# Additions to the output between GpSimd's weight splits, and the tiles without rows moved ahead of the fifth expert's

## The chip, the cores and the metric

The kernel runs on one core of one Trainium2 chip. The metric is the device time of one execution in microseconds, lower is better, given as the median of several runs. Profiles show one execution each: TensorE (PE, weight loads PEld), VectorE (DVE), ScalarE (ACT), GpSimd (POOL) and the sync engine (SP), each with its own instruction queue, and 16 DMA engines that all queues share.

## The reference

16 samples of 69 tokens of width 256 (a class token, 36 image patches, 32 text tokens; 1104 tokens) pass a patch embedding, one attention layer and one layer of experts. The last is what the change touches:

```
h = h + ffn(layernorm(h))
ffn(x): shared = expert(x, shared_up, shared_down)              # all tokens
        probs  = softmax(x @ router_w)                          # 8 routed experts
        gates  = the two largest probs of each token, else 0
        routed = sum over e of gates[e] * expert(x, routed_up[e], routed_down[e])
        return shared + routed + x
expert(x, up, down) = gelu(x @ up) @ down                       # 256 -> 1024 -> 256
```

## The kernel before, in words

**Stages.** Patch embedding and attention take the first third. The shared expert runs over all tokens while the router's result is turned into a table. Then the routed experts run over tiles of 128 rows, each row a (token, expert) pair.

**Tiles.** `TILES` is 25, the most that 2208 pairs over 8 experts can need; each expert's rows fill whole tiles, one expert after another. `rtab[:, 1]` is each expert's number of tiles, `rtab[:, 2]` the scan of it (the tile at which each expert ends), `rtab[:, 3]` where it starts. Tiles that no expert needs stand at the end; their rows all point at 128 spare rows behind the output, and their gates are zero. They are computed like the others, with the last expert's weights. `etab` gives each tile its expert, `eplace` the expert's turn in the ring of weights.

**TensorE.** Step `s` of `run_steps` transposes tile s+2's rows, makes tile s+1's up product (L876 to L878 with `xgT`, after a wait on `w_ready` for its expert's turn), turns tile s's hidden values, and makes tile s-1's down product. VectorE multiplies it by the gates into `xy_all[:, t]` (L1418) and raises `y_ready`.

**GpSimd** runs one queue, written out by hand. `prepare_half(x, part)` splits half an expert's weights (up, then down; 2048 elements a partition) from `stage` into a high part (L394) and a low part (L395) in the ring of four experts' places, then issues the load of the next expert's same half (L384). For x above 4 it first waits for the tiles of the expert whose place it takes. x = 0 is the shared expert, x = 1 to 8 the routed ones. `gather_rows` (L502) reads a tile's 128 normalized rows by an indirect DMA; the sync engine then copies them to `xg` (L355), from which TensorE transposes. `add_rows` (L512) adds a tile's results to the output's rows in HBM by an indirect DMA with addition. Two experts may hold the same token, so an addition must not run beside another expert's: `additions[t]` (made on VectorE up to L1370) is the count of `y_out` that it waits for (L509), the end of the experts before its own; a tile without rows waits for all additions before it, since all use the same spare rows. It also waits for its own result (L511). In the kernel before, all 25 additions stand behind the last split.

**VectorE** makes the tables while TensorE works on the shared expert, in a chain in which each instruction waits for the last (`link`), with the shared expert's own steps (L1228, on which TensorE waits) between them: the scan L1320, the subtraction L1321, later `etab`, `eplace` and `additions`.

Of the kernel before, what the change touches and what calls it, by code (L numbers as in the profile page):

```python
# [9 lines left out]
ALU = mybir.AluOpType  # L10
# [3 lines left out]
P = 128  # L14

NB, NPATCH, NTXT, D, F, NE = 16, 36, 32, 256, 1024, 8
# [27 lines left out]
TILES = (2 * T - 1) // P + NE  # L44
CAP = -(-T // P)
RING = 4
HB = 5
EW = 2 * KD * F
UPW = KD * F
NX = NE + 1  # L50
GROUPS_OF = [-(-min(SN * (q + 1), T) // GT) for q in range(NSG)]
FREE_ROWS = 13

S_VALID, S_RANK, S_THR, S_TILE = 0, NT, NT + NE, NT + NE + CAP
S_TOK = S_TILE + TILES
# [5 lines left out]
def fusion_layer(nc, patches, txt, cls_token, cls_pos, ln1_gb, tok_w, tok_bias, ln2_g, ln2_b,  # L61
# [5 lines left out]
    def sb(name, shape, dt=F32, where=ctx, side="left"):  # L67
        return where.enter_context(nc.sbuf_tensor(name, shape, dt, side=side))

    def sem(name):  # L70
        return ctx.enter_context(nc.semaphore(name))
# [5 lines left out]
    with ctx:  # L77
# [6 lines left out]
        stage = sb("stage", [P, 2, UPW])  # L84
        rsm = sb("rsm", [P, 8, NT])
        rtab = sb("rtab", [P, 4, NE])
        etab = sb("etab", [P, TILES])
        ecmp = sb("ecmp", [P, TILES * NE])
        eplace = sb("eplace", [1, TILES], I32)
        ekeep = sb("ekeep", [1, 2, TILES])  # L90
        ytab = sb("ytab", [1, 2, TILES])
# [44 lines left out]
        n = KP * D  # L136
# [91 lines left out]
        w_free, w_ready = sem("w_free"), sem("w_ready")  # L228
# [5 lines left out]
        r_additions = sem("r_additions")  # L234
# [136 lines left out]
        def _(pool):  # L371
            link_count = [0]

            def link(ins):
                link_count[0] += 1
                ins.then_inc(s_pool, 1)
                pool.wait_ge(s_pool, link_count[0])

            def load_weights(n):

                if n < 2 * NX:
                    if n >= 2:
                        pool.wait_ge(w_free, n - 1)
                    pool.dma_start(stage[:, n % 2, :], (w_up, w_dn)[n % 2][n // 2, :, :]).then_inc(w_in[n % 2], 16)  # L384

            def tiles_before(x):

                return pool.value_load(tend_int[0:1, x - 1:x], min_val=0, max_val=TILES)

            def split(x, part, c0, c1):  # L390

                pool.wait_ge(w_in[part], 16 * (x + 1))
                hi, lo = (ring[:, x % RING, v, UPW * part + c0:UPW * part + c1] for v in range(2))
                link(nc.gpsimd.tensor_scalar(hi, stage[:, part, c0:c1], 1.0, 0.0, ALU.mult, ALU.add))  # L394
                return nc.gpsimd.tensor_tensor(lo, stage[:, part, c0:c1], hi.bitcast(F32), ALU.subtract)  # L395

            def turn_done(x):

                pool.wait_ge(w_free, 2 * x + 2)
                pool.sem_inc(w_ready, 4)  # L400

            def prepare_half(x, part):

                if x > RING and part == 0:

                    pool.wait_ge(ffn_done, tiles_before(x - RING) + 1)
                    pool.sem_inc(slot_free, 1)
                elif x in (RING - 1, RING) and part == 0:

                    pool.wait_ge(ffn_done, 1)  # L410
                split(x, part, 0, UPW).then_inc(w_free, 1)
                if part == 1:
                    turn_done(x)
                load_weights(2 * x + part + 2)
# [45 lines left out]
            n = TROWS[NPT - 1]  # L460
# [37 lines left out]
            def gather_rows(t0, t1):  # L498
                for t in range(t0, t1):
                    if t >= 4:  # L500
                        pool.wait_ge(rows_in[t % 4], 16 * (t // 4))
                    pool.indirect_dma_start(  # L502
                        xy_all[:, t, :], None, xn_d,
                        bass.IndirectOffsetOnAxis(ap=dest[:, t:t + 1].bitcast(U32), axis=0)).then_inc(rows_in[t % 4], 16)

            def add_rows(t0, t1):
                for t in range(t0, t1):
                    if t >= 1:
                        pool.wait_ge(y_out, pool.value_load(additions[0:1, t:t + 1], min_val=16, max_val=16 * TILES))  # L509
                        pool.sem_inc(rows_free, 1)  # L510
                    pool.wait_ge(y_ready, t + 1)  # L511
                    pool.indirect_dma_start(out, bass.IndirectOffsetOnAxis(ap=dest[:, t:t + 1].bitcast(U32), axis=0),  # L512
                                            xy_all[:, t, :], None, compute_op=ALU.add).then_inc(y_out, 16)
# [9 lines left out]
            turn_done(2)  # L523
            gather_rows(10, FREE_ROWS)
            prepare_half(3, 0)
            prepare_half(3, 1)
            pool.wait_ge(base_out, 16 * (NSG + 1))
            gather_rows(FREE_ROWS, FREE_ROWS + 2)
            prepare_half(4, 0)
            gather_rows(FREE_ROWS + 2, FREE_ROWS + 4)  # L530
            prepare_half(4, 1)
            gather_rows(FREE_ROWS + 4, FREE_ROWS + 6)


            t = FREE_ROWS + 6
            for x in range(RING + 1, NX):
                for part in range(2):
                    prepare_half(x, part)
                    n = min(t + 2, TILES)
                    gather_rows(t, n)  # L540
                    t = n
            pool.wait_ge(r_additions, 1)
            add_rows(0, TILES)


        @block.scalar
# [507 lines left out]
        def _(dve):  # L1054
            v = nc.vector
            link_count = [0]

            def link(ins):

                link_count[0] += 1  # L1060
                ins.then_inc(s_dve, 1)
                dve.wait_ge(s_dve, link_count[0])
# [255 lines left out]
                                 small[:, S_THR:S_THR + CAP].unsqueeze(1).to_broadcast([P, NE, CAP]), ALU.is_gt))  # L1318
            link(v.tensor_reduce(rtab[:, 1, :], c3, AX.X, ALU.add))
            link(v.tensor_tensor_scan(rtab[:, 2, :], small[:, S_ONE:S_ONE + NE], rtab[:, 1, :], 0.0, ALU.mult, ALU.add))  # L1320
            link(v.tensor_tensor(rtab[:, 3, :], rtab[:, 2, :], rtab[:, 1, :], ALU.subtract))  # L1321
            link(v.tensor_scalar(rtab[:, 3, :], rtab[:, 3, :], float(P), None, ALU.mult))
            link(v.tensor_tensor(n3(rout[:, 5, :]), n3(ps[:, 6, 0:NE * NT]),
# [2 lines left out]
            for k in range(2):  # L1326
                link(v.tensor_tensor(rout[:, 6 + k, :], rout[:, 5, :], rpick[:, k, :], ALU.mult))
                last = v.tensor_reduce(slot[:, NT * k:NT * (k + 1)], n3(rout[:, 6 + k, :]), AX.X, ALU.add)
# [35 lines left out]
            tile_no = small[0:1, S_TILE:S_TILE + TILES]  # L1364
            link(v.tensor_tensor(e3[0:1], e3[0:1], rtab[0:1, 2, :].unsqueeze(1).to_broadcast([1, TILES, NE]), ALU.mult))
            link(v.tensor_reduce(ytab[:, 0, :], e3[0:1], AX.X, ALU.max))
            link(v.scalar_tensor_tensor(out=ytab[:, 1, :], in0=tile_no, scalar=rtab[0:1, 2, NE - 1:NE], in1=tile_no,
                                        op0=ALU.is_ge, op1=ALU.mult))
            link(v.tensor_tensor(ytab[:, 0, :], ytab[:, 0, :], ytab[:, 1, :], ALU.max))
            v.tensor_scalar(additions[:, :], ytab[:, 0, :], 1.0, 16.0, ALU.max, ALU.mult).then_inc(r_additions, 1)  # L1370
# [105 lines left out]
```

## Time and profile before

| | |
|---|---|
| median of 3 runs | 371.01 us (368.86 to 376.37) |
| the profiled execution | 370.01 us |
| its span | 368.2 us |
| busy PE, PEld | 309.9 us (84%), 276.5 us (75%) |
| busy DVE, ACT | 159.5 us (43%), 152.5 us (41%) |
| busy POOL | 201.6 us (55%), 151 instructions |
| granted TensorE clock, mean | 0.943 of full speed |
| DMA, mean over the span | 107 GB/s |

The span runs from the first to the last record of the profile; the execution's own time is a little longer. Busy shares are means over stages with different limits, so the rows below go by stretch and by instruction. In a row of instructions the number in square brackets is how long the engine was idle before it, and behind the arrow is what ended that.

### The profile page before, as it was taken

The numbers are of one execution on the slowest core, as the hardware profiler recorded it, in microseconds if no ns is written. First come the engines' busy times: TensorE is split into PE (matmuls) and PEld (weight loads), VectorE is DVE, ScalarE is ACT, GpSimd is POOL, SyncE is SP. The second block draws the span as 40 slices with busy tenths as digits, with TensorE's granted clock in tenths as the row PEclk, the third lists the DMA queues.
The fourth block names the chain that finished last, engine by engine and source line by source line (L and its number), as shares of the span: only waits on it lengthen the run. The fifth ranks groups of instructions, "written<-read, shape, count | busy, mean of one in ns | idle before, by whom it ended". The sixth has DMA issues, their size and how long they took to land.

```text
span 368.2 us, 6657 instructions
## 1 busy us (share of the span) xinstructions
PE 309.9 (84%) x2063; PEld 276.5 (75%) x2064; DVE 159.5 (43%) x394; ACT 152.5 (41%) x327; POOL 201.6 (55%) x151
## 2 busy tenths in 40 slices
PE   1787487899849898999899999999999999999700
PEld 1565266788639687999698999999989999999600
DVE  3344738899662339764232332333323323323200
ACT  2364421656786644354243434334334343342100
POOL 1332202854848000257789988889998355563531
PEclk9989678999967999999999999999999999999975
DMA  7944010031451431057344444443440444443321
GB/s 249 267 138 154 15 50 1 2 114 64 141 196 56 151 98 56 16 154 291 108 142 162 158 159 168 157 170 110 147 142 14 57 72 57 61 53 43 35 30 22
DMA packets 21358, 39.39 MB, mean 107 GB/s; under 512 B 2856, under 2 KB 17659, under 8 KB 19035
## 3 DMA queue, kind: packets, MB, share of 16 engines
q0 software_dynamic: 7392, 25.43, 26.1%
q1 hardware_dynamic: 13658, 13.51, 12.1%
q8 instruction: 11, 0.18, 0.2%
q10 hardware_dynamic: 288, 0.20, 0.2%
q14 instruction: 9, 0.07, 0.1%
HBM read 28.32 MB, written 6.93 MB: 96 GB/s over the span
## 4 chain that ended last, share of the span: by engine, by line
POOL 27%; PE 25%; DMA 14%; issue 12%; DVE 11%; ACT 4%; POOLq 3%; SPq 3%; PEldq 0%; DVEq 0%
POOL ring L395 15%; DMA out_tokens<-xy_all,dest 12%; PE ps L927 7%; POOL ring L394 6%; PE ps L876 4%; PE ps L878 3%; PE ps L877 3%; PE ps L783 3%; POOL xy_all L502 3%; POOLq L509 2%; PE ps L847 1%; PE ps L755 1%; POOL stage L384 1%; DVE h L1164 1%; DMA clsr<-in_cls_pos 1%
## 5 line engine op out<-in xcount | busy, mean ns | idle before, releaser
L395 POOL TENSOR_TENSOR ring<-stage,ring 128x512 fp32r<-128x512 f32 (+1 forms) x28 | 75.8, 2706 | 2.3
L1412 DVE TENSOR_TENSOR hgT<-ps,hgT 128x512 fp32r<-128x512 f32 x50 | 32.2, 686 | 71.6 <-ACT hgT L745 71.6
L512 POOL DMA_INDIRECT out_tokens<-xy_all,dest x25 | 39.1, 1564 | 40.5 <-DMA out_tokens<-xy_all,dest 30.3
L876 PE MATMUL ps<-ring,hgT 128*128 x200 | 58.6, 293 | 2.1 <-DVE xy_all L1418 1.5
L877 PE MATMUL ps<-ring,hgT 128*128 x200 | 56.6, 283 | 0.0
L878 PE MATMUL ps<-ring,hgT 128*128 x200 | 56.5, 283 | 0.0
L737 ACT ACTIVATE hg<-ps 128x512 f32<-128x512 f32 x50 | 29.9, 598 | 47.0 <-PE ps L878 47.0
L502 POOL DMA_INDIRECT xy_all<-normalized_tokens,dest x25 | 24.7, 989 | 42.4 <-DVE dest L1374 35.1
L876 PE MATMUL ps<-ring,xgT 128*128 x100 | 41.0, 410 | 1.1 <-issue 0.6
L876 PEld LDWEIGHTS ps<-ring,hgT 128*128 128x128 f32 x200 | 38.2, 191 | 2.6 <-issue 2.6
L878 PE MATMUL ps<-ring,xgT 128*128 x100 | 39.1, 391 | 0.0
L877 PE MATMUL ps<-ring,xgT 128*128 x100 | 39.1, 391 | 0.0
L877 PEld LDWEIGHTS ps<-ring,hgT 128*128 128x128 f32 x200 | 38.4, 192 | 0.0
L878 PEld LDWEIGHTS ps<-ring,hgT 128*128 128x128 f32 x200 | 38.3, 192 | 0.0
L394 POOL TENSOR_SCALAR ring<-stage 128x512 fp32r<-128x512 f32 (+1 forms) x28 | 32.9, 1175 | 3.1 <-PEq L1004 2.5
L720 ACT ACTIVATE xgT<-ps 128x256 fp32r<-128x256 f32 x25 | 9.6, 385 | 55.1 <-PE ps L755 55.1
L927 PE MATMUL ps<-ring,hid 128*128 128x256 f32 x216 | 30.2, 287 | 0.2 <-DVE base L1236 0.2
L1418 DVE TENSOR_SCALAR xy_all<-ps,gate 128x256 f32 (+1 forms) x25 | 12.1, 484 | 40.1 <-PE ps L878 40.1
L927 PEld LDWEIGHTS ps<-ring,hid 128*128 128x128 f32 x216 | 29.1, 194 | 0.5 <-issue 0.5
L745 ACT ACTIVATE hgT<-ps 128x512 fp32r<-128x512 f32 x50 | 27.1, 599 | 2.7 <-PE ps L755 2.7
L755 PE MATMUL ps<-mats,hg 128*128 128x128 f32 x200 | 25.9, 272 | 0.0
L755 PEld LDWEIGHTS ps<-mats,hg 128*128 128x128 f32 x200 | 23.3, 140 | 3.1
(178 smaller groups left out, 600.9 us busy)
## 6 DMA issues: line engine op xcount, KB each, us to landing
stage<-in_w_up POOLq DMA_DIRECT2D x9, 1024.0 KB, 5.3
stage<-in_w_dn POOLq DMA_DIRECT2D x9, 1024.0 KB, 5.5
xg<-xy_all SPq DMA_DIRECT2D x25, 128.0 KB, 2.1
xp<-in_patches SPq DMA_DIRECT2D x4, 384.0 KB, 5.5
normalized_tokens<-hn SPq DMA_DIRECT2D x4, 276.0 KB
residual_tokens<-h SPq DMA_DIRECT2D x4, 276.0 KB
ring<-in_tok_w SPq DMA_DIRECT2D x1, 768.0 KB, 6.2
base<-residual_tokens SPq DMA_DIRECT2D x2, 384.0 KB, 3.6
```

Of the source, the lines that this page charges most:

```text
L394: link(nc.gpsimd.tensor_scalar(hi, stage[:, part, c0:c1], 1.0, 0.0, ALU.mult, ALU.add))
L395: return nc.gpsimd.tensor_tensor(lo, stage[:, part, c0:c1], hi.bitcast(F32), ALU.subtract)
L502: pool.indirect_dma_start(xy_all[:, t, :], None, xn_d, bass.IndirectOffsetOnAxis(ap=dest[:, t:t + 1].bitcast(U32), axis=0)).then_inc(rows_ ...
L512: pool.indirect_dma_start(out, bass.IndirectOffsetOnAxis(ap=dest[:, t:t + 1].bitcast(U32), axis=0), xy_all[:, t, :], None, compute_op=ALU. ...
L737: nc.scalar.activation(hg[:, 1 - c, 512 * half:512 * (half + 1)], ps[:, hidden_bank + half, :], ACT.Gelu).then_inc(e_act, 1)
L745: nc.scalar.activation(hgT[:, c, 0, 4 * half:4 * half + 4, :], ps[:, turned_bank + half, :].rearrange("p (k t) -> p k t", k=4), ACT.Copy). ...
L755: return nc.tensor.transpose(o, i, ident[0:n, 0:n])
L876: nc.tensor.matmul(o, a[0], b[0], start=n == 0, stop=False)
L877: nc.tensor.matmul(o, a[0], b[1], start=False, stop=False)
L878: last = nc.tensor.matmul(o, a[1], b[0], start=False, stop=n == len(pairs) - 1)
L927: last = nc.tensor.matmul(ps[:, down_bank[j], 0:D], a[x], b[y], start=f == 0 and m == 0, stop=f == KF - 1 and m == 2)
L1412: v.tensor_tensor(hgT[:, c, 1, 4 * half:4 * half + 4, :], ps[:, turned_bank + half, :].rearrange("p (k t) -> p k t", k=4), hgT[:, c, 0, 4 ...
```

## The change

GpSimd's queue is written anew from the fourth routed expert on. The additions of tiles 0 to 10 stand between the splits (one each around the fifth, sixth and seventh expert's halves, then two, two and one); the last expert's two halves are split in two pieces each, with additions between; tiles 11 to 24 follow behind the last piece. The wait for `r_additions` moves ahead of the gather of tile 13. The gathers keep their order, and the same two stand behind the same halves.

On VectorE the number of unused tiles is computed (`unused`), and added to the ends of the experts from the fifth on, so that the tiles without rows lie between the fourth and the fifth expert and use the fifth expert's weights. The table of additions is made to fit: a tile without rows waits for all before it, the fifth expert's tiles wait for the tiles without rows too.

```diff
+EMPTY_AT = 4
...
+        unused = sb("unused", [P, 1])
...
-            def prepare_half(x, part):
+            def prepare_half(x, part, c0=0, c1=UPW):
-                if x > RING and part == 0:
+                if x > RING and part == 0 and c0 == 0:
...
-                split(x, part, 0, UPW).then_inc(w_free, 1)
+                last = split(x, part, c0, c1)
+                if c1 < UPW:
+                    return
+                last.then_inc(w_free, 1)
...
             pool.wait_ge(base_out, 16 * (NSG + 1))
-            gather_rows(FREE_ROWS, FREE_ROWS + 2)
+            pool.wait_ge(r_additions, 1)
+            gather_rows(13, 15)
             prepare_half(4, 0)
-            gather_rows(FREE_ROWS + 2, FREE_ROWS + 4)
+            gather_rows(15, 17)
             prepare_half(4, 1)
-            gather_rows(FREE_ROWS + 4, FREE_ROWS + 6)
-            t = FREE_ROWS + 6
-            for x in range(RING + 1, NX):
-                for part in range(2):
-                    prepare_half(x, part)
-                    n = min(t + 2, TILES)
-                    gather_rows(t, n)
-                    t = n
-            pool.wait_ge(r_additions, 1)
-            add_rows(0, TILES)
+            gather_rows(17, 19)
+            add_rows(0, 1)
+            prepare_half(5, 0)
+            gather_rows(19, 21)
+            add_rows(1, 2)
+            prepare_half(5, 1)
+            gather_rows(21, 23)
+            add_rows(2, 3)
+            prepare_half(6, 0)
+            gather_rows(23, 25)
+            prepare_half(6, 1)
+            add_rows(3, 4)
+            prepare_half(7, 0)
+            add_rows(4, 5)
+            prepare_half(7, 1)
+            add_rows(5, 6)
+            prepare_half(8, 0, 0, UPW // 2)
+            add_rows(6, 8)
+            prepare_half(8, 0, UPW // 2, UPW)
+            add_rows(8, 10)
+            prepare_half(8, 1, 0, UPW // 2)
+            add_rows(10, 11)
+            prepare_half(8, 1, UPW // 2, UPW)
+            add_rows(11, TILES)
...
             link(v.tensor_tensor_scan(rtab[:, 2, :], ...))
+            link(v.tensor_scalar(unused[:, :], rtab[:, 2, NE - 1:NE], -1.0, float(TILES), ALU.mult, ALU.add))
+            link(v.tensor_scalar(rtab[:, 2, EMPTY_AT:], rtab[:, 2, EMPTY_AT:], unused[:, :], None, ALU.add))
...
-            link(v.scalar_tensor_tensor(out=ytab[:, 1, :], in0=tile_no, scalar=rtab[0:1, 2, NE - 1:NE], in1=tile_no,
+            first = rtab[0:1, 2, EMPTY_AT - 1:EMPTY_AT]
+            link(v.tensor_tensor(unused[0:1, :], unused[0:1, :], first, ALU.add))
+            link(v.tensor_scalar(ytab[:, 1, :], tile_no, unused[0:1, :], None, ALU.min))
+            link(v.scalar_tensor_tensor(out=ytab[:, 1, :], in0=tile_no, scalar=first, in1=ytab[:, 1, :],
                                         op0=ALU.is_ge, op1=ALU.mult))
```

## Rows read from the trace of the kernel before

**Rows 1.** The page, part 4: the chain that ended last, by engine.

```profile
POOL 27%; PE 25%; DMA 14%; issue 12%; DVE 11%; ACT 4%; POOLq 3%; SPq 3%; PEldq 0%; DVEq 0%
```

**Rows 2.** Stretches: us, busy PE, PEld, DVE, ACT, POOL, clock, DMA, GB/s.

```profile
186.00:340.00 154.00, 154.00 (x1058) 141.68 (x1057) 50.91 (x93) 58.99 (x116) 117.13 (x62) 1.00 0.42 111
...
349.70:368.20 18.50, 0.00 (x0) 0.00 (x0) 0.00 (x0) 0.00 (x0) 4.67 (x3) 0.61 0.22 26
```

**Rows 3.** VectorE in order of time: results of tiles 0, 22, 23, 24.

```profile
192.61 0.49 DVE L1418 TENSOR_SCALAR xy_all<-ps,gate 128x256 f32<-128x256 f32 x1 [1.34 <-PE ps L878]
...
339.95 0.48 DVE L1418 TENSOR_SCALAR xy_all<-ps,gate 128x256 f32<-128x256 f32 x1 [1.33 <-PE ps L878]
...
344.56 0.48 DVE L1418 TENSOR_SCALAR xy_all<-ps,gate 128x256 f32<-128x256 f32 x1 [2.20 <-PE ps L878]
349.21 0.48 DVE L1418 TENSOR_SCALAR xy_all<-ps,gate 128x256 f32<-128x256 f32 x1 [4.16 <-PE ps L878]
```

**Rows 4.** GpSimd in order of time: additions 0, 1, 2 and the last.

```profile
283.65 1.67 POOL L512 DMA_INDIRECT out_tokens<-xy_all,dest  x1 [0.94 <-POOL ring L395]
288.42 1.57 POOL L512 DMA_INDIRECT out_tokens<-xy_all,dest  x1 [3.10 <-DMA out_tokens<-xy_all,dest]
290.29 1.57 POOL L512 DMA_INDIRECT out_tokens<-xy_all,dest  x1 [0.30 <-issue]
...
360.76 1.56 POOL L512 DMA_INDIRECT out_tokens<-xy_all,dest  x1 [2.98 <-DMA out_tokens<-xy_all,dest]
```

**Rows 5.** Waits of the additions (total us, times, longest), and their landing.

```profile
POOL out_tokens L512 <- DMA out_tokens<-xy_all,dest: 30.3, 11, 3.1
...
POOL out_tokens L512 <- DVE xy_all L1418: 5.9, 2, 3.0
```
```profile
DMA to landing us min/median/max: 3.6/3.8/4.0
```

**Rows 6.** GpSimd in order of time: the fifth expert's halves, the last split.

```profile
214.34 0.95 POOL L502 DMA_INDIRECT xy_all<-normalized_tokens,dest  x1 [0.30 <-issue]
215.33 1.93 POOL L394 TENSOR_SCALAR ring<-stage 128x2048 fp32r<-128x2048 f32 x1
217.34 4.62 POOL L395 TENSOR_TENSOR ring<-stage,ring 128x2048 fp32r<-128x2048 f32 x1
222.26 0.60 POOL L384 DMA_DIRECT2D stage<-in_w_up  x1 [0.30 <-POOL ring L395]
...
227.47 4.62 POOL L395 TENSOR_TENSOR ring<-stage,ring 128x2048 fp32r<-128x2048 f32 x1
...
278.08 4.63 POOL L395 TENSOR_TENSOR ring<-stage,ring 128x2048 fp32r<-128x2048 f32 x1
```

**Rows 7.** GpSimd's groups by form, splits of 512 elements: busy us, mean ns.

```profile
L395 POOL TENSOR_TENSOR ring<-stage,ring 128x512 fp32r<-128x512 f32 x16 | 20.4, 1278 | 1.3
L394 POOL TENSOR_SCALAR ring<-stage 128x512 fp32r<-128x512 f32 x16 | 9.8, 615 | 0.0
```

**Rows 8.** TensorE in order of time: first up products of tiles 10, 23.

```profile
239.49 0.48 PE L876 MATMUL ps<-ring,xgT 128*128 x1
```
```profile
326.68 0.48 PE L876 MATMUL ps<-ring,xgT 128*128 x1
```

**Rows 9.** Landing of six gathers (190 to 216 us), of ten loads (180 to 270).

```profile
DMA to landing us min/median/max: 2.0/4.5/5.3
```
```profile
DMA to landing us min/median/max: 5.0/5.3/5.8
```

**Rows 10.** The chain of waits, start and us: VectorE's table, TensorE behind it.

```profile
139.78 0.19 DVE rtab L1320
...
139.98 0.18 DVE rtab L1321
...
144.48 0.41 PE ps L876
```

## The prediction

> **What bounds the kernel now.** I read the chain of waits first, then the stretches of the end, then GpSimd's and VectorE's instructions in order of time. The chain is led by GpSimd and by the additions' transfers [rows 1], which says that the end hangs on the queue that issues them. The stretches say where: from 186 to 340 us TensorE is busy for the whole of 154.00 us at full granted clock and waits for nothing, and from 349.7 us to the end no engine computes, 18.5 us in all [rows 2]. VectorE writes the scaled result of tile 0 at 193.1, then one about every 6.7 us: tile 22 at 340.43, tile 23 at 345.04, tile 24 at 349.69 [rows 3]. GpSimd issues its first addition only at 283.65, when its last weight split is over, and the last at 360.76 [rows 4]. So two things run side by side, TensorE's tiles (over at 349.69) and GpSimd's queue (last addition 11.07 us later), and the queue sets the end. An addition that may follow at once starts 1.87 us after the one before it; one that waits for the landing of the one before starts about 4.54 us after it (1.56 busy and 2.98 idle) [rows 4]. The landing takes 3.8 us [rows 5], so about 0.8 us of each such step is GpSimd's own way from the release to the start. There are twelve such waits of 2.8 to 3.1 us (the thirteenth in the groups is one of 0.30) [rows 5], and 12 x 4.54 + 12 x 1.87 = 76.9 is the 77.1 us from first to last.
>
> The tiles at which the waits stand (1, 3, 6, 8, 10, 13, 17, 19, then 21, 22, 23 and 24 one by one) give the experts' tile counts, 3, 3, 2, 2, 3, 4, 2, 2, and four tiles without rows. Routing by the reference on these inputs gives the same.
>
> **The sum.** The profiled execution took 370.01 us, its span is 368.2, so 1.8 us lie outside; it stands 1.0 us under the median of the three runs, 371.01.
>
> *Additions put between the splits.* Eleven of the 25 go ahead of GpSimd's last split. All their results are long there (tile 10's at about 260 us, its addition near 301), and every landing they wait for has a split of 6.6 us or half a one in between. What an addition costs GpSimd between other instructions, no row shows. From below: 1.56 us, its busy time with nothing beside. From above: 1.67 + 0.94 = 2.6, the first addition's busy time with the idle time ahead of it, behind a split [rows 4]; further off, 4.54 if it held the engine until it lands. The nearest rows are the gathers, the same kind of instruction in the same places: 0.3 us idle ahead, and the split starts 0.04 us after the gather's end, though a gather takes up to 5.3 us to land [rows 6, 9]. I take 2.1 (1.67 and some 0.4) for one alone and 3.9 for two together: additions 0 to 5 make 12.6, 6 and 7 with 8 and 9 make 7.8, 10 makes 2.0; 22.4 in all.
>
> *The last expert in four pieces.* Each half is cut in two. A pair of instructions on 512 elements takes 0.62 + 1.28, on 2048 it takes 1.93 + 4.62 [rows 6, 7]; four small ones would be 7.6 against 6.55, so a cut costs about 0.35 and a start gap of 0.1. Two cuts: 0.9. The end of the last split goes from 282.7 [rows 6] to 282.7 + 22.4 + 0.9 = 306.0.
>
> *Does TensorE wait for weights?* The fifth expert's second half ended at 227.47 + 4.62 = 232.1; two additions now stand ahead of it, so 236.3. The first product with that slot is tile 10's, at 239.49 [rows 6, 8]: 3.2 us to spare, now for a tile without rows. This is the tightest place; at 2.6 us an addition it still has 2.2. The next experts' slots are wanted four tiles, 26.8 us, later than before. The last expert's is wanted with tile 23, at 326.68 [rows 8], and is there at 306.0. Loads, gathers and the transfers that the sync queue starts from them only slide with GpSimd: each load lands in 5.0 to 5.8 us [rows 9] and has a half's turn of over 8 us ahead of its use; the last gather, near 251, is for a tile transposed after 326.5. They cost nothing, and would show as waits of a split for its load if that cover were gone.
>
> *The additions behind the last split.* Addition 11 starts 0.9 behind it, at 306.9. The tiles without rows are now 10 to 13, each waiting for the one before, then the experts have 3, 4, 2 and 2 tiles. So from 11 to 24 there are six waiting steps (12, 13, 14, 17, 21, 23) and seven free ones: 6 x 4.54 + 7 x 1.87 = 40.3, and addition 24 could start at 347.2. Its result is there only at 349.69. Here is the gain: it starts on the result, not on the queue. Behind the release I add the same 0.8 us: 350.5. The queue is 3.3 us ahead of that, so costs that I set too low by that much are free. (Tile 22's result at 340.43 holds addition 22 until 341.2, which leaves 24 free at 347.6; it does not decide.) From the last start to the end of the span are 368.2 - 360.76 = 7.44 us: 357.9.
>
> *VectorE's small instructions.* Two are put into the table's chain between the scan and the subtraction, each at the spacing of 0.20 us that such ones have (139.78 to 139.98), and TensorE's products wait for that chain at 144.48 [rows 10]; from there on TensorE runs without a gap that could take it back. I take 0.4 us for the whole, with 0 and 0.8 as ends. Two more in the table of additions lie beside TensorE's own table products; they may push the first gathers by 0.3, with some 20 us until tile 0's transposition. The new one-element tile may move the tiles after it by some bytes, for which I take nothing. Both clocks, TensorE's and GpSimd's, start from TensorE's end of the shared expert, so all of the above shifts alike. Span 358.3, execution 360.1: 9.9 under the profiled one, or 361.1 if the same is taken off the median. I say 360.6.
>
> *A page weighed.* The gathers that stand behind a weight load landed in 2.0 to 5.3 us [rows 9], beside 3.8 for additions with no load about [rows 5]; the only addition that is followed closely by a dependent one behind a load is 5, with 5.5 us until 6, so by the rows it is just covered. The Trainium skill (DMA: Bandwidth & Descriptors, section "Issuing engines are not separate DMA queues") says that all issued transfers interleave on the same 16 engines, and its section "Anatomy of one DMA" fits 2.0 us plus bytes over 436 GB/s, about 4.4 us for 1 MB, where the trace has 5.0 or more. An addition behind a whole load would by that page's data term (an estimate) land 2.4 us later, at 6.2, and addition 6 would be 0.7 us late, within the 3.3 of cover; it speaks against the change only as a small push toward the first rival.
>
> **Rivals.**
> *GpSimd comes late.* Starts behind a load or a split cost more, or transfers wait on each other. At 2.6 us an addition the queue is 11 x 0.5 = 5.5 later, 2.2 past its cover: 362.8. Only from 5.8 us (0.53 an addition) is less than 2% left; with twice that, 366 to 367. For: the 0.94 us that the first addition stood idle. Against: the gathers' 0.3.
> *An addition holds GpSimd until it lands.* 4.54 instead of 2.1 each, 11 times: 26.8 us. The fifth expert is ready at 241.2, so TensorE stops 1.7 us at tile 10; the last is ready at 332.8, addition 11 starts at 333.7, 24 at 374.0, and the execution takes 374.0 + 7.44 + 0.4 + 1.8 = 383.6, 13.6 slower. Over 2% slower it is from about 4.0 us an addition. Against it: free additions follow at 1.87 while landing takes 3.8, and splits start right behind gathers in flight. For: no split behind an addition in flight has a row.
> *The empty tiles do not move.* Were the count of unused tiles zero in effect, the last expert would be wanted with tile 19, at 299.85 by the 6.7 us spacing, and be ready at 306.0: TensorE ends 6.2 us later, and the execution is 366.3. The four lone waits at the end of the old queue speak against.
>
> **How the numbers follow.** The forecast, end on tile 24's result: 0.78. GpSimd late: 0.12, of it half still over 2% faster. Additions that hold the engine: 0.04. Empty tiles unmoved: 0.02. Not named, a slower stretch of TensorE or transfers in each other's way: 0.04. About 2% is what a measurement of this kernel can tell from no change, 7.4 us, so faster means under 363.6. That gives faster 0.81, same 0.14, slower 0.05. Range: below, the start 0.7 earlier, no cost on VectorE and the profiled level, 359.0, and a little for the runs' scatter: 358.0. Above, GpSimd late and the unmoved tiles: 366.5.
>
> **What would show it.** Right: the last addition starts within 1 us of tile 24's result; TensorE shows no wait from 186 to 340; the last split ends near 306; each interleaved addition takes 2.0 to 2.6 us from the end of the instruction before to the start of the next; the idle end is 8.3 us and not 18.5. Wrong: a wait of tile 10's first product, splits that start only on an addition's landing, or a last addition released by another addition and not by VectorE.

## The result, and the profile after

The changed kernel takes 360.51 us (median of 4 runs, 357.18 to 361.61), the kernel before 370.75 (4 runs). The ratio is 0.972, with a 95% interval of 0.967 to 0.977: 2.8% faster. The median forecast was 360.6. The profiled execution took 360.22 us, its span is 358.4. A second set of runs later gave 360.17 us (6 runs) and 0.970 (0.966 to 0.975). Some executions run in a slower state (376.37 us for the kernel before); the ratios leave these out.

The stretches, with the columns of [rows 2]:

```profile
186.00:340.00 154.00, 154.00 (x1061) 140.85 (x1060) 50.78 (x92) 60.06 (x118) 123.67 (x69) 1.00 0.44 113
350.69:358.40 7.71, 0.00 (x0) 0.00 (x0) 0.01 (x1) 0.00 (x0) 1.56 (x1) 0.77 0.22 28
```

From 186 to 340 us TensorE is busy without a gap, as before, and the stretch behind the last result, 18.5 us in [rows 2], is 7.7. VectorE's results of tiles 0, 22, 23 and 24, against [rows 3]:

```profile
194.39 0.48 DVE L1445 TENSOR_SCALAR xy_all<-ps,gate 128x256 f32<-128x256 f32 x1 [1.28 <-PE ps L900]
...
341.06 0.48 DVE L1445 TENSOR_SCALAR xy_all<-ps,gate 128x256 f32<-128x256 f32 x1 [1.27 <-PE ps L900]
...
345.62 0.48 DVE L1445 TENSOR_SCALAR xy_all<-ps,gate 128x256 f32<-128x256 f32 x1 [2.15 <-PE ps L900]
350.21 0.48 DVE L1445 TENSOR_SCALAR xy_all<-ps,gate 128x256 f32<-128x256 f32 x1 [4.11 <-PE ps L900]
```

GpSimd in order of time: addition 0 and the first split behind it, addition 3 behind a load, addition 6 to the last piece's end, additions 11 and 12, and the last two. It answers to [rows 4, 6].

```profile
216.17 0.95 POOL L507 DMA_INDIRECT xy_all<-normalized_tokens,dest  x1 [0.30 <-issue]
217.42 1.63 POOL L517 DMA_INDIRECT out_tokens<-xy_all,dest  x1 [0.30 <-issue]
218.51 2.50 POOL L396 TENSOR_SCALAR ring<-stage 128x2048 fp32r<-128x2048 f32 x1
...
233.16 4.61 POOL L397 TENSOR_TENSOR ring<-stage,ring 128x2048 fp32r<-128x2048 f32 x1
...
260.90 0.61 POOL L386 DMA_DIRECT2D stage<-in_w_dn  x1 [0.59 <-POOL ring L397]
262.27 1.63 POOL L517 DMA_INDIRECT out_tokens<-xy_all,dest  x1 [0.76 <-DVE xy_all L1445]
263.37 2.48 POOL L396 TENSOR_SCALAR ring<-stage 128x2048 fp32r<-128x2048 f32 x1
...
282.47 1.62 POOL L517 DMA_INDIRECT out_tokens<-xy_all,dest  x1 [0.77 <-DVE xy_all L1445]
...
288.33 1.60 POOL L517 DMA_INDIRECT out_tokens<-xy_all,dest  x1 [0.66 <-issue]
290.24 1.56 POOL L517 DMA_INDIRECT out_tokens<-xy_all,dest  x1 [0.30 <-issue]
291.25 1.66 POOL L396 TENSOR_SCALAR ring<-stage 128x1024 fp32r<-128x1024 f32 x1
...
305.49 2.40 POOL L397 TENSOR_TENSOR ring<-stage,ring 128x1024 fp32r<-128x1024 f32 x1
309.37 1.58 POOL L517 DMA_INDIRECT out_tokens<-xy_all,dest  x1 [1.48 <-DVE xy_all L1445]
313.84 1.57 POOL L517 DMA_INDIRECT out_tokens<-xy_all,dest  x1 [2.89 <-DMA out_tokens<-xy_all,dest]
...
347.95 1.56 POOL L517 DMA_INDIRECT out_tokens<-xy_all,dest  x1 [3.00 <-DMA out_tokens<-xy_all,dest]
350.97 1.56 POOL L517 DMA_INDIRECT out_tokens<-xy_all,dest  x1 [1.46 <-DVE xy_all L1445]
```

Three things are to be seen. A split starts 1.09 us after the addition ahead of it (1.0 to 1.1 for all of them), while the addition is still at work, and its first instruction takes 2.50 us instead of 1.93: the two overlap. The last split ends at 307.89. And the last addition was released by VectorE: it starts 0.28 us after tile 24's result, having stood idle for 1.46 us, where 0.30 is what a free one shows.

TensorE's first up product of tile 10, for which the fifth expert's slot (ready at 233.16 + 4.61 = 237.8) must be there, starts at 241.08 behind no wait, so 3.3 us were to spare.

### The profile page after: what moved, and what is told of

It reads as the page before. It is cut to its first block, busy times and chain, and to the rows that moved or that the text cites. A ratio compares the mean times of both kernels' runs of the same rounds, so it can differ in the third digit from the quotient of the medians.

```text
span 358.4 us, 6664 instructions
## 1 busy us (share of the span) xinstructions
PE 309.5 (86%) x2063; PEld 275.4 (77%) x2064; DVE 160.0 (45%) x398; ACT 152.5 (43%) x327; POOL 203.3 (57%) x155
## 4 chain that ended last, share of the span: by engine, by line
PE 42%; POOL 13%; DVE 12%; issue 12%; DMA 11%; ACT 3%; POOLq 3%; SPq 1%; DVEq 0%
DMA out_tokens<-xy_all,dest 10%; PE ps L898 8%; PE ps L900 8%; PE ps L899 8%; PE ps L949 7%; POOL ring L397 6%; PE ps L777 5%; PE ps L805 3%; POOL ring L396 3%; POOL out_tokens L517 2%; POOLq L514 2%; PE ps L869 2%; DVE h L1186 1%; PE ps L1012 1%; DVE st L1194 1%
## 5 line engine op out<-in xcount | busy, mean ns | idle before, releaser
L397 POOL TENSOR_TENSOR ring<-stage,ring 128x512 fp32r<-128x512 f32 (+2 forms) x30 | 76.1, 2536 | 2.5
L898 PE MATMUL ps<-ring,hgT 128*128 x200 | 58.0, 290 | 2.1 <-DVE xy_all L1445 1.5
L900 PE MATMUL ps<-ring,hgT 128*128 x200 | 55.9, 279 | 0.0
L899 PE MATMUL ps<-ring,hgT 128*128 x200 | 55.9, 279 | 0.0
L396 POOL TENSOR_SCALAR ring<-stage 128x512 fp32r<-128x512 f32 (+2 forms) x30 | 38.5, 1283 | 2.7 <-PEq L1026 2.5
L898 PEld LDWEIGHTS ps<-ring,hgT 128*128 128x128 f32 x200 | 37.6, 188 | 2.6 <-issue 2.6
L899 PEld LDWEIGHTS ps<-ring,hgT 128*128 128x128 f32 x200 | 37.7, 188 | 0.0
L900 PEld LDWEIGHTS ps<-ring,hgT 128*128 128x128 f32 x200 | 37.6, 188 | 0.0
L777 PEld LDWEIGHTS ps<-mats,hg 128*128 128x128 f32 x200 | 23.3, 140 | 3.2
```

What stands on the lines that cost most here:

```text
L777: return nc.tensor.transpose(o, i, ident[0:n, 0:n])
L898: nc.tensor.matmul(o, a[0], b[0], start=n == 0, stop=False)
L899: nc.tensor.matmul(o, a[0], b[1], start=False, stop=False)
L900: last = nc.tensor.matmul(o, a[1], b[0], start=False, stop=n == len(pairs) - 1)
```

## A measure free of the early stages' scatter

Between executions the shared expert's first addition to `base` starts anywhere from 135.1 to 140.2 us, whatever the kernel, and the medians carry part of that. So each profile is read in three stretches: A from that addition to the start of tile 0's result, B from there to tile 24's result, C from there to the end of the span. The table has all profiles, and beside them each kernel's median.

| kernel | A | B | C | median, us |
|---|---|---|---|---|
| before | 55.22 | 156.60 | 18.99 | 370.75 |
| changed | 55.61 | 155.82 | 8.19 | 360.51 |
| e1 additions only | 55.17 | 165.83 | 8.84 | 370.16 |
| e2 empty tiles only | 55.60 | 155.84 | 19.37 | 370.85 |
| e3 whole halves | 57.12 * | 155.83 | 11.29 | 362.13 |
| e4 queue late | 55.60 | 155.84 | 10.80 | 360.81 |
| e5 more between | 55.61 | 155.84 | 8.99 | 359.43 |
| e6 longer chain | 57.29 * | 155.84 | 8.18 | 361.65 |
| e7 parts first | 58.77 * | 155.84 | 8.19 | 361.76 |
| e8 the same, table later | 54.35 | 155.85 | 8.20 | 359.01 |
| e9 tile only | 56.20 | 155.96 | 19.60 | 371.60 |
| e10 before again | 58.87 * | 156.60 | 18.87 | one run, 372.3 |
| e11 changed again | 56.77 | 155.85 | 8.18 | 360.17 |
| e12 as e8, again | 54.42 | 155.85 | 8.17 | 358.69 |

The star marks profiles in which the granted clock fell between 130 us and tile 0's result. B and C repeat to 0.1 us; A does where the clock stays at full and VectorE's second three additions to `base` (at about 164 us) aren't late. In e9 and e11 they start 2.12 and 2.31 us after the instruction before them instead of 1.1, and TensorE waits 1.2 and 1.4 us for it; in the kernel before and the changed one it waits 0.2. The loads for `base` had landed some 20 us earlier, so what was late isn't known.

## The experiments

### Additions only (e1)

The changed kernel without these lines, and with the table of additions made as in the kernel before:

```diff
-            link(v.tensor_scalar(unused[:, :], rtab[:, 2, NE - 1:NE], ...))
-            link(v.tensor_scalar(rtab[:, 2, EMPTY_AT:], rtab[:, 2, EMPTY_AT:], unused[:, :], None, ALU.add))
```

> The additions between the splits and the pieces of the last expert stay, the tiles without rows stand at the end again (VectorE's new instructions are gone). Theory: the additions push the last split to about 307.5 us, and the last expert is wanted with tile 19, at about 301; TensorE stops there for 6 to 7 us and its end moves by as much, and so does the time: 366 to 368 us, 6 to 7 above the changed kernel, still under the kernel before. Rival (the place of the empty tiles does nothing, all of the gain is the moved additions): 360 to 361 us, TensorE without a wait.

Measured: 370.16 us (10 runs), ratio to the kernel before 1.000 (0.996 to 1.005). The wait is where it was expected and as long, but the time is 2 to 4 us above the 366 to 368 that I expected. TensorE's waits from 186 to 350 us (total, times, longest), and its instructions around tile 19:

```profile
PE ps L898 <- POOLq L402: 7.0, 1, 7.0
```

```profile
306.99 0.79 PE L898 MATMUL ps<-ring,xgT 128*128 x1 [6.96 <-POOLq L402]
307.57 0.63 PE L899 MATMUL ps<-ring,xgT 128*128 x1
...
311.84 0.63 PE L900 MATMUL ps<-ring,xgT 128*128 x1
312.27 1.42 PE L777 MATMUL ps<-mats,hg 128*128 128x128 f32 x8
```

But B is 10.0 us longer, not 7. The stretches say why (columns as in [rows 2]):

```profile
186.00:300.00 114.00, 114.00 (x787) 104.21 (x785) 38.05 (x70) 44.48 (x88) 100.22 (x55) 1.00 0.46 136
300.00:309.00 9.00, 2.04 (x6) 1.63 (x6) 0.91 (x2) 0.38 (x1) 7.29 (x5) 0.66 0.17 29
309.00:320.00 11.00, 11.00 (x62) 9.55 (x61) 2.20 (x4) 3.76 (x7) 6.94 (x5) 0.82 0.45 60
320.00:345.00 25.00, 25.00 (x175) 22.94 (x173) 8.36 (x15) 9.08 (x19) 8.65 (x6) 1.00 0.30 37
```

The engine had stood for 7.0 us, and came back on a lower granted clock: 0.50 from 307 to 311 us, the 1.2 GHz level instead of 2.4. The twelve up products start 0.43 us apart (the first two 0.58), 4.85 us from 306.99 to 311.84, where at the full clock they are 0.23 apart and take 2.6. With the last of them, the turned hidden values behind them (1.42 us instead of 1.03) and 0.2 us of overlap lost at the stop it makes 3.0 us more. Another 0.65 is in C: addition 24 now waited for 23's landing. So moving the additions alone is worth nothing here: what it takes from the queue it gives back as a stop of TensorE, 7.0 us, and 3.0 more, nearly all for the clock.

### Empty tiles only (e2)

The kernel before with VectorE's part of the change alone; GpSimd's queue is the old one.

```diff
+            link(v.tensor_scalar(unused[:, :], rtab[:, 2, NE - 1:NE], -1.0, float(TILES), ALU.mult, ALU.add))
+            link(v.tensor_scalar(rtab[:, 2, EMPTY_AT:], rtab[:, 2, EMPTY_AT:], unused[:, :], None, ALU.add))
```

> The tiles without rows stand ahead of the fifth expert's, GpSimd's queue is that of the kernel before, all additions behind the last split. Theory: twelve waits for a landing remain, only at other tiles, so the additions still take 77 us from the end of the last split: 370.5 to 371.5 us, no difference from the kernel before beyond 0.4 us for VectorE's chain. Rival (the empty tiles at the end, waiting one by one, were what made the tail long): 365 us or less.

Measured: 370.85 us (10 runs), ratio 1.003 (0.998 to 1.008). C is 19.37 beside 18.99, and B with C, from tile 0's result to the end, 175.2 beside 175.6: twelve waits for a landing are twelve wherever they stand. The rival is out. With e1 it shows that neither half of the change does anything alone, and both together take 10 us.

### Whole halves of the last expert (e3)

```diff
-            prepare_half(8, 0, 0, UPW // 2)
-            add_rows(6, 8)
-            prepare_half(8, 0, UPW // 2, UPW)
-            add_rows(8, 10)
-            prepare_half(8, 1, 0, UPW // 2)
-            add_rows(10, 11)
-            prepare_half(8, 1, UPW // 2, UPW)
-            add_rows(11, TILES)
+            prepare_half(8, 0)
+            add_rows(6, 10)
+            prepare_half(8, 1)
+            add_rows(10, TILES)
```

> The changed kernel with the last expert's halves whole, additions 6 to 9 between them and 10 to 24 behind. Theory: the cuts let additions 8 and 10 wait under a split; without them GpSimd stops some 2.7 us between the halves for the landing of 7 and then a whole step of 4.5 us for 11 behind 10, less 0.9 for the two cuts and 2 for addition 10; the queue comes 3.8 us later than in the changed kernel, of which about 1.2 are covered by the wait for tile 24's result: 2.6 us slower, 362.5 to 363.5. Rival (the cuts are only overhead, the queue is far ahead of the results, as the prediction's 3.3 us had it): 360 to 361.

Measured: 362.13 us (4 runs, 360.53 to 365.75), ratio 0.983 (0.970 to 0.997). The runs overlap those of the changed kernel, C does not: 11.29 against 8.19, 3.1 us more, where 2.6 was expected (addition 23 waited 3.64 us for a landing and not 3.0). The wait between the halves is there (2.98 us idle), and the last addition starts behind number 23 after the 0.30 us of a free one: no result holds it. GpSimd in order of time:

```profile
292.44 1.56 POOL L517 DMA_INDIRECT out_tokens<-xy_all,dest  x1 [0.30 <-issue]
296.98 1.57 POOL L517 DMA_INDIRECT out_tokens<-xy_all,dest  x1 [2.98 <-DMA out_tokens<-xy_all,dest]
...
351.84 1.56 POOL L517 DMA_INDIRECT out_tokens<-xy_all,dest  x1 [3.64 <-DMA out_tokens<-xy_all,dest]
353.70 1.56 POOL L517 DMA_INDIRECT out_tokens<-xy_all,dest  x1 [0.30 <-issue]
```

### Queue late (e4)

```diff
             prepare_half(8, 1, UPW // 2, UPW)
+            for _ in range(2):
+                link(nc.gpsimd.tensor_scalar(stage[:, 0, :], stage[:, 0, :], 1.0, 0.0, ALU.mult, ALU.add))
             add_rows(11, TILES)
```

> The changed kernel with two more GpSimd instructions behind the last split, each a multiplication of a stage half by one (2048 elements, 1.92 us), ahead of additions 11 to 24: the queue comes 3.9 us later. Theory from the profile of the changed kernel: the last addition stood idle 1.46 us for tile 24's result where 0.30 would do, so 1.2 us are covered and 2.7 show: 363.0 to 363.5. By the prediction's cover of 3.3 us only 0.6 would show: 361. If the queue set the end, all 3.9: 364.4.

Measured: C 10.80, so 2.6 us of the 3.9 show and 1.3 were covered, as the profile's 1.2 said, and not the prediction's 3.3. The time does not settle it: 360.81 us (6 runs, 359.35 to 364.26), where the two accounts had 363.0 to 363.5 and 361, lies in the changed kernel's own scatter. C does: A and B of this profile are the changed kernel's. The two instructions and the last two additions of that profile:

```profile
309.68 3.93 POOL L566 TENSOR_SCALAR stage<-stage 128x2048 f32<-128x2048 f32 x2 [0.20 <-POOL ring L397]
...
353.15 1.56 POOL L517 DMA_INDIRECT out_tokens<-xy_all,dest  x1 [3.01 <-DMA out_tokens<-xy_all,dest]
355.01 1.56 POOL L517 DMA_INDIRECT out_tokens<-xy_all,dest  x1 [0.30 <-issue]
```

### More between (e5)

```diff
+            add_rows(3, 4)
             prepare_half(6, 1)
-            add_rows(3, 4)
+            add_rows(4, 5)
             prepare_half(7, 0)
...
             prepare_half(8, 0, 0, UPW // 2)
-            add_rows(6, 8)
+            add_rows(7, 9)
             prepare_half(8, 0, UPW // 2, UPW)
-            add_rows(8, 10)
+            add_rows(9, 11)
             prepare_half(8, 1, 0, UPW // 2)
-            add_rows(10, 11)
+            add_rows(11, 12)
             prepare_half(8, 1, UPW // 2, UPW)
-            add_rows(11, TILES)
+            add_rows(12, TILES)
```

> The changed kernel with twelve additions instead of eleven ahead of the last split (number 3 moves between the gathers of tiles 23 and 24 and the sixth expert's second half, the others follow one place earlier, number 11 goes ahead of the last piece). Theory: the queue behind the last split has one waiting step of 4.5 us less and starts 2.5 us later, so it is about 2 us further ahead of the results, and the end stays on tile 24's result: from tile 0's result to the span's end 164.0 us as in the changed kernel, within 0.3, and addition 24 idle some 3 us ahead of its start instead of 1.46. Rival (the queue still sets part of the end): 1 to 2 us less.

A miss. C is 8.99, 0.8 us longer than the changed kernel's; the time, 359.43 us (4 runs, 358.12 to 363.49), does not tell them apart. I had counted the additions and not the boundaries: in pairs 7, 8 and 9, 10 the second belongs to the next expert (10 to an empty tile) and waits in front of the splits.

```profile
288.62 1.60 POOL L517 DMA_INDIRECT out_tokens<-xy_all,dest  x1 [0.16 <-issue]
293.14 1.55 POOL L517 DMA_INDIRECT out_tokens<-xy_all,dest  x1 [2.92 <-DMA out_tokens<-xy_all,dest]
...
298.40 1.58 POOL L517 DMA_INDIRECT out_tokens<-xy_all,dest  x1
303.07 1.57 POOL L517 DMA_INDIRECT out_tokens<-xy_all,dest  x1 [3.09 <-DMA out_tokens<-xy_all,dest]
...
350.56 1.56 POOL L517 DMA_INDIRECT out_tokens<-xy_all,dest  x1 [0.30 <-issue]
```

That is 5.4 us more than two free pairs, and with the twelfth addition the last split ends 6.9 us later against tile 0's result. The additions behind it take 4.9 us less. So the queue is 2.0 us later, 1.2 of it covered, and 0.8 shows: it sets the end again, the last addition having come free. The order of the changed kernel puts a piece of a split ahead of each of these.

### Longer chain (e6)

```diff
+            for _ in range(8):
+                link(v.tensor_scalar(rtab[:, 2, EMPTY_AT:], rtab[:, 2, EMPTY_AT:], 0.0, None, ALU.add))
```

> The changed kernel with eight more small instructions in VectorE's chain behind the new ones (each adds zero to four elements a partition). Theory: each costs 0.26 us and TensorE waits for that chain, so 2.1 us more from the first addition to base (shared expert, first three) to tile 0's result, 57.7 us instead of 55.6, and 2.1 us in the time. Rival (TensorE's waits for VectorE in that stage take it in): 0.5 us or less.

Measured: A 57.29, 1.7 us more, 0.21 for each of the eight; 361.65 us (4 runs). Expected were 2.1 us, at 0.26 each. In VectorE's order of time the eight take 1.63 us (141.74 to 143.37). The clock fell in this profile too (0.88 from 136 to 150 us), and how the 1.7 parts between the two stays open; the rival's 0.5 does not fit the 1.63, and the two instructions of the change itself cost 0.39 in A (55.61 against 55.22; 55.17 in e1, which lacks them) at a full clock.

### Parts of the shared expert first (e7, e8, e12)

Parts 11, 12 and 13 also stand where 10, 11 and 12 stood. The last two pairs of lines are in e8 and e12 only.

```diff
-            shared_parts(8, 9)
+            shared_parts(8, 10)
             shared_end(0, SG)
-            shared_parts(9, 10)
+            shared_parts(10, 11)
...
-        LANES, TABLE, TABLE_AT = 128, 256, 15
+        LANES, TABLE, TABLE_AT = 128, 256, 16
...
-                else:
+                elif n < 7:
```

> The changed kernel with VectorE's subtraction of the shared expert's part 9 ahead of the three additions to base, in a stretch where VectorE was idle for 5.3 us, and parts 10 to 13 each one place earlier in its queue. Theory: TensorE's waits for these parts (1.7, 0.4 and 0.8 us) go, but it then waits for the table's chain, which ends only some 0.5 us earlier: 0.5 to 1 us less from the first addition to base to tile 0's result. Rival (those waits are what delays the stage): 2.5 to 3 us less.

> As the run before, and TensorE's product of the table one step of the shared expert later (behind step 15 instead of 14), which gives TensorE 2.1 us of work while VectorE ends the chain. Theory: now the waits go without a new one in their place, 2 to 2.9 us less from the first addition to base to tile 0's result, 52.7 to 53.6 us instead of 55.6, and as much in the time: about 358 us. Rival (VectorE's chain also holds later parts): under 1 us.

> The version with parts of the shared expert earlier in VectorE's queue and the table's product one step later, beside the changed kernel. By the profile of its first run, 1.26 us less ahead of tile 0's result: 359.2 us, ratio 0.968. If that was only a stretch without a fall of the clock: 360.5.

> The changed kernel as it is, beside the next one on the same chip. 360.5 us, ratio 0.972; 55.6 us from the first addition to base to tile 0's result, unless the granted clock falls in that stretch.

In e7 the waits only changed names. TensorE's waits from 100 to 180 us in the changed kernel, then in e7, then in e8:

```profile
PE ps L898 <- DVE hid L1250: 6.8, 5, 2.2
```

```profile
PE ps L898 <- DVE hid L1250: 4.3, 3, 1.8
PE ps L1012 <- DVE in_lane L1372: 2.4, 1, 2.4
```

```profile
PE ps L898 <- DVE hid L1250: 4.3, 3, 1.8
...
PE ps L949 <- DVE base L1258: 1.3, 2, 1.1
```

6.8 became 4.3 + 2.4, next to nothing gained, where 0.5 to 1 us was expected; and A was 3.2 us longer, with the granted clock at 0.77 from 150 to 165 us. With the table's product a step later 1.4 us of waits are gone, and A is 54.35 and 54.42, 1.2 us less than the changed kernel's 55.61. I had expected 2 to 2.9: 4.3 us of waits for the parts stay, and one for `base` grows from 0.2 to 1.3. In the changed kernel's second profile (e11) A is 56.77 at the full clock, where 55.6 was expected: it is one of the two with late additions to `base`. The times are 359.01 (6 runs) and 358.69 us (6 runs, ratio 0.967, 0.963 to 0.971), beside 360.17 for the changed kernel on the same chip (0.970, 0.966 to 0.975). It is the quickest version of all by both medians and by A, but the intervals of the ratios overlap.

### The new tile alone (e9), and the kernel before again (e10)

```diff
+        unused = sb("unused", [P, 1])
         etab = sb("etab", [P, TILES])
```

> The kernel before with nothing but the new one-element tile, allotted where the change allots it and used by nothing. From tile 0's result to tile 24's the kernel before took 156.60 us and every profile with the change's tile 155.84 (but for one run that stopped for weights). Theory: the tile shifts the addresses of those behind it, and the down products run a little closer: 155.84 us here too. Rival (the order of additions or of the tiles without rows does it, or it is the execution's scatter): 156.6. The time stays at the kernel before's, 370 to 372 us, in either case, since the additions set its end.

> The kernel before as it is, for a second profile. By the theory of the shifted addresses 156.60 us from tile 0's result to tile 24's again, within 0.1; by scatter of the execution, something else. From the first addition to base to tile 0's result 55.2 us.

B is 156.60 in both profiles of the kernel before (A in the second is 58.87 and not 55.2: the clock fell there), and 155.96 with a tile that nothing uses, 155.82 to 155.85 in all the others with it that didn't stop. So the order of the work has no part in most of it. The down products (durations in ns, min/median/max), before and after:

```profile
L877 PE MATMUL ps<-ring,hgT x152: 282/283/283, 203.1 to 326.3; 128*128 x152
```

```profile
L899 PE MATMUL ps<-ring,hgT x155: 277/278/282, 199.9 to 327.5; 128*128 x155
```

The 24 of a tile start within 2.83 us before (236.40 to 239.23) and 2.77 after (238.05 to 240.82, and 2.77 in e9 too), 0.06 less; the up products ahead of them take some ns more in the changed kernel (393 instead of 389 in the median for one line). The rest is 0.03 us a tile and 0.7 in B. That it comes through the addresses of the tiles behind the new one is what is left, but it is argued: no run moved them by other amounts, so the rule behind it stays open. e9's time, 371.60 us, is the kernel before's: the queue set the end.

## Why the prediction was right

**The bound and its removal: right.** The end is now tile 24's result plus one addition; TensorE waits nowhere from 186 to 340 us; the idle end is 7.7 us where 8.3 was forecast and 18.5 stood before. Runs e1 and e2 show both halves to be needed.

**The cost of the eleven additions: right in sum, by another make-up.** Forecast 22.4 us and 0.9 for the cuts, 23.3 in all. From tile 0's result the last split's end went from 282.71 - 192.61 = 90.10 to 307.89 - 194.39 = 113.50: 23.4. An addition behind gathers costs 1.35 us more until the split starts (1.39 between gather and split, 0.04 before) and 0.57 for the stretched instruction, 1.9; one behind a load 2.3 to 2.4, since it starts 0.76 us behind the load and not 0.3.

**The rivals.** GpSimd does not stand still until the landing: splits start 1.09 us after an addition begins while it lands in 3.7 to 5.1 us. The unmoved tiles were priced at 366.3 us and took 370.2 in e1. The step that failed there is the sum of that rival, in which a stop of TensorE cost its own length: 6.2 us forecast and 7.0 found, and then 3.0 for the clock and 0.65 for addition 24 behind 23.

**The cover of 3.3 us: too large, 1.2.** Three terms. First, the queue came 0.8 us later against tile 0's result (349.82 - 194.39 = 155.4, when addition 24 could have gone, against 347.2 - 192.6 = 154.6), of which 0.5 is the idle time ahead of addition 11, 1.48 and not 0.94. Second, the tiles ran 0.8 us quicker over B, which nobody forecast. Third, the way from the result to the addition is 0.28 us, not the 0.8 that I took over from the landing; why it is shorter no run shows. Runs e3, e4 and e5 fit a cover of 1.2. The chain from 11 to 24 was 40.4, forecast 40.3.

**VectorE's chain: 0.39, forecast 0.4.**

**The total.** 358.3 was forecast and 358.4 found, closer than the terms are. Against the forecast, stretch A began 1.4 us late by scatter, and B with C were 1.3 us shorter by the second and third of the three terms above. That these cancel is luck, and so is 0.8 us of the gain itself: the prediction took nothing for the new tile, and B is shorter by it. Stretch by stretch the change is worth 11 us ((55.22 + 156.60 + 18.99) - (55.61 + 155.82 + 8.19) = 11.2), and 10.2 by the medians.

**The estimate by the Trainium skill.** By the Trainium skill (DMA: Bandwidth & Descriptors, section "Anatomy of one DMA") the prediction put addition 5 behind its load at 6.2 us, an estimate, and addition 6 at 0.7 us late. That left out the 0.8 us from a landing to the next start, with which it would be 1.5. Addition 5 landed in 5.0 us, 1.2 above the 3.8 of one with no load about, and 6 stood idle 0.66 us, 0.5 more than number 8 with a free way (0.15). So the push is real, but the data term of the Trainium skill, 2.4 us for the whole load, is too much here.

## What to carry to other kernels

When a queue sets the end, look what else it feeds: work moved forward in it pushes the rest back, and the gain is real only if the deadlines behind it are moved too (here by putting useless tiles where they buy time). Count dependent steps, not steps: an addition that waits for a landing costs 4.5 us by itself and about 2 where a split covers the wait, so the boundary between experts, not the number, says where it belongs. And a stop of TensorE can cost more than its length (10.0 us for 7.0 in e1).

## What the runs showed of the hardware that was not expected

- After a stop of 7.0 us TensorE's granted clock was 0.50, its products ran at little over half their rate for about 5 us, and the stop cost 10.0 us (e1). The Trainium skill (TensorE: Matmul & The Clock Gate, section "Part 1: The HAM clock gate") has the two levels of 1.2 and 2.4 GHz. The trace agrees: 0.50 granted, and a spacing of 0.43 against 0.23 us, a ratio of 1.9.
- The clock also fell in some executions of unchanged code in the shared expert's stage, at 150 to 160 us (0.66 in e10, 0.83 in e3), and A was 1.5 to 3.7 us longer there. It fell without a longer stop ahead of it: TensorE's waits from 125 to 160 us in e10 are 2.5 us, 1.7 the longest, as in the first profile of the kernel before, whose clock stays at full, and the engine was busy for all of 150 to 160. What made it fall no run shows. It may be a good part of what the medians scatter by: in e11 the executions with a mean granted clock of 0.960 took 357.55 and 357.94 us, that with 0.943 took 362.01.
- A GpSimd instruction on 2048 elements a partition that follows an indirect addition starts 1.09 us into it and takes 0.57 us more (2.50 and not 1.93).
- One unused element a partition, allotted among the tiles, made stretch B 0.64 us shorter (156.60 to 155.96 in e9).
